# Normalising with the mean itself instead of a negated copy, in a one-core attention and expert kernel

## Chip, cores and metric

The kernel runs on one core of one Trainium2 chip. The metric is device time in microseconds (us), from start to end of one execution. A core has TensorE (PE, with its weight loads shown apart as PEld), VectorE (DVE), ScalarE (ACT), GpSimd (POOL) and SyncE (SP, which only issues DMAs here).

## The reference

One layer on x of 8 batches, 256 rows each, 256 features. The attention half is `x = x + LN(attention(LN(x)))` with 16 query heads, 4 key heads, head size 128, a layer norm and a rotation of q and k, a causal softmax and an output projection. The second half is `x = x + LN(ffn(LN(x)))`, where ffn is a top-2 choice of 8 experts and one shared expert. The plain layer norm of both halves has no gain:

```python
def _layernorm(x, axis=-1, eps=1e-05):
    m = jnp.mean(x, axis=axis, keepdims=True)
    v = jnp.var(x, axis=axis, keepdims=True)
    return (x - m) / jnp.sqrt(v + eps)
```

Everything is fp32. On TensorE each product is made of three passes (lines L460, L461, L462) over high and low parts of the operands, which is why DVE has many subtractions that make low parts (lines with W as output).

## The kernel before

All of x stays in SBUF as X, 128 rows by 256 columns in each of 16 tiles. The order of work of every engine is written out by hand, and the engines meet through semaphores. A woven loop over slots s = 0 to 128 carries the attention: slot by slot one head's scores, softmax, transposes, value product and output projection, and beside it the projection, norm and rotation of q and k of a coming (batch, key head) group. One such group has two units u, one for each tile of 128 rows. After slot 128 the tail of the attention is woven with the router, the scatter of rows to the experts and the first items of the shared expert; then come the expert tiles and the last norms.

Two of the layer norms are touched here, each once for a batch b of two tiles:

- ln1, before the attention. DVE takes statistics (`ln1_stats`, L1346 and L1350), which leaves mean and variance side by side in the tile `mv`, slots 0 and 1. POOL makes the factor 1/sqrt(var+eps) (`ln1_root`, L2005 to L2007, through `root`, L2000 and L2002) in the tile `lr`. Then X is normalised into `hrow`: by DVE for batch 0 (`ln1_apply`, L1358) and by POOL for batches 1 to 7 (`ln1_apply`, L2040). In the loop the POOL root stands in slot 16b-10 and the POOL apply in slot 16b-5.
- the norm of the attention's output, in place in `osb`: statistics on DVE (`out_stats`, L1488 and L1492) into slots 2 and 3 of `mv`, root on POOL (`out_root`, L2056 to L2058), scaling by POOL for batches 0 to 5 (`out_scale`, L2047) and by DVE for batches 6 and 7 (L1498), then the addition to X (`out_add`).

On POOL these stand in one queue with `rope(u)`, four large or middling operations for each unit (L2002, L2016, L2019, L2026) and one small one (L2000), and later with the scatters (`scatter`, L2111, an indirect DMA issued by POOL). POOL's form of the normalisation adds a negated mean, which it first makes in a tile of its own, `nm`; DVE's form of the same subtracts the mean in `mv`. The router's work on DVE after the loop (`route_count`, `place_own`, `place_ends`, L1631 to L1669) stands ahead of `out_scale(6)` and of `pv_lo(58)` (L1478), which makes an operand that TensorE needs.

Of the kernel before, what the change touches and what calls it, by code (L numbers as in the profile page):

```python
# [5 lines left out]
ALU = mybir.AluOpType  # L6
# [109 lines left out]
def program(nc, x_d, wqkv_d, wo_d, gb_d, sw_d, ew_d, cs_d, const_d, route_d, spare_d, out_d):  # L116
    with ExitStack() as ctx:
        def sb(name, shape, dt=F32):
            return ctx.enter_context(nc.sbuf_tensor(name, shape, dt))
# [4 lines left out]
        def sem(name):  # L124
            return ctx.enter_context(nc.semaphore(name))
# [10 lines left out]
        X = sb("X", [128, NT, HID])  # L136
# [20 lines left out]
        hrow = sb("hrow", [128, 2, HID])  # L157
        p_flat = sb("P", [128, 1536])
        P = p_flat[:, :].rearrange("p (z c) -> p z c", z=4)
        osb = sb("osb", [128, 2, HID])  # L160
# [7 lines left out]
        st = sb("st", [128, 4, 6])  # L168
        mv = sb("mv", [128, 4, 2])
        lr = sb("lr", [128, 4])  # L170
        nm = sb("nm", [128, 4])
        nmx = sb("nmx", [128, 4, 2])
        sums = sb("sums", [128, 4, 2])
        rinv = sb("rinv", [128, 4, 2])
# [37 lines left out]
        for c, (a, b) in enumerate(CHUNKS):  # L212
# [60 lines left out]
                for (a, b), p in zip(CHUNKS, (pQ[:, 768:1024], pS[1], pS[1]))]  # L273
# [44 lines left out]
        s_bn, s_aggr, s_hrow, s_hT, s_wsum, s_wmean_d, s_wcen, s_wqlo_d, s_tab_d, s_rope_d = (  # L318
            sem(n) for n in ("s_bn", "s_aggr", "s_hrow", "s_hT", "s_wsum", "s_wmean_d", "s_wcen", "s_wqlo_d",
                             "s_tab_d", "s_rope_d"))  # L320
# [5 lines left out]
        s_obn, s_oaggr, s_oscale, s_res = (sem(n) for n in ("s_obn", "s_oaggr", "s_oscale", "s_res"))  # L326
# [1669 lines left out]
        def _(e):  # L1996
            def root(n, src, dst, scale, s_of, s_variance, s_root, k):

                e.wait_ge(*s_of)
                e.tensor_scalar(dst, src, scale, EPS, ALU.mult, ALU.add).then_inc(s_variance, 1)  # L2000
                e.wait_ge(s_variance, k + 1)
                e.tensor_tensor(dst, dst, half[:, 0:n], ALU.pow).then_inc(s_root, 1)  # L2002

            def ln1_root(b):
                e.wait_ge(s_aggr, b + 1)  # L2005
                e.tensor_scalar(nm[:, 0:2], mv[:, 0:2, 0], -1.0, None, ALU.mult)
                root(2, mv[:, 0:2, 1], lr[:, 0:2], 1.0, (s_aggr, b + 1), s_var, s_lr, b)  # L2007

            def rope(u):
# [26 lines left out]
            def ln1_apply(b):  # L2036
                e.wait_ge(s_lr, b + 1)
                e.wait_ge(s_ln1T, b)
                for t in range(2):
                    a = e.tensor_scalar(hrow[:, t, :], X[:, 2 * b + t, :], nm[:, t:t + 1], lr[:, t:t + 1], ALU.add,  # L2040
                                        ALU.mult)
                a.then_inc(s_hrow, 1)

            def out_scale(b):
                e.wait_ge(s_olr, b + 1)
                for t in range(2):
                    a = e.tensor_scalar(osb[:, t, :], osb[:, t, :], nm[:, 2 + t:3 + t], lr[:, 2 + t:3 + t], ALU.add,  # L2047
                                        ALU.mult)
                a.then_inc(s_oscale, 1)

# [2 lines left out]
                e.tensor_tensor(X[:, 2 * b:2 * b + 2, :], X[:, 2 * b:2 * b + 2, :], osb[:, :, :], ALU.add).then_inc(s_res, 1)  # L2053

            def out_root(b):
                e.wait_ge(s_oaggr, b + 1)  # L2056
                e.tensor_scalar(nm[:, 2:4], mv[:, 2:4, 0], -1.0, None, ALU.mult)
                root(2, mv[:, 2:4, 1], lr[:, 2:4], 1.0, (s_oaggr, b + 1), s_ovar, s_olr, b)  # L2058

            def norm_root(k):  # L2060
# [110 lines left out]
            e.memset(half[:, :], -0.5).then_inc(s_half, 1)  # L2171
            e.wait_ge(s_half, 1)
            ln1_root(0)
            e.wait_ge(s_wqhi, 1)
            e.tensor_tensor(WQ[:, 0, 1, 0, :], raw_q[0][:, 0, :], f(WQ[:, 0, 0, 0, :]),
# [9 lines left out]
            for s in range(WOVEN):  # L2185
                if s == 2:
                    rope(0)
                if QFIRST <= s <= 2 * NU and (s - 1) % 2 == 1:
                    rope((s - 1) // 2)
                if s % 16 == 6 and s // 16 + 1 < NB:  # L2190
                    ln1_root(s // 16 + 1)
                fb, fs = divmod(s - LATE - 15, 16)
                if s % 16 == 11 and s // 16 + 1 < NB:
                    ln1_apply(s // 16 + 1)
                if 0 <= fb < NB - 1 and fs == 1:
                    out_root(fb)
                if 0 <= fb < NB - 2 and fs == 2:
                    out_scale(fb)
                if 0 <= fb < NB - 2 and fs == 4:
                    out_add(fb)  # L2200
                if 0 <= fb < NB - 2 and fs == 7:
                    ln2_root(fb)
                if s == ZERO:
                    row_ends()
                if s - 1 in SWHI[0:2]:
                    sw_lo(SWHI.index(s - 1))
# [37 lines left out]
            scatter(1, 11, 0)  # L2244
            scatter(1, 11, 1)
            out_root(7)
            e.wait_ge(s_uact, 4)
            scatter(1, 12, 0)
# [82 lines left out]
```

## Time and profile before

| what | value |
|---|---|
| median of 3 runs | 675.61 us (675.12 to 675.86) |
| the profiled execution's own time | 675.86 us |
| its span, first to last instruction | 673.9 us |
| mean granted TensorE clock | 0.977 of full speed |
| busy PE / DVE / ACT / POOL | 628.6 / 564.9 / 563.8 / 541.8 us |
| instructions on POOL | 606 |

The span is 1.96 us shorter than the time of the same execution; that rest lies outside the first and last instruction. Busy time of an engine says how full it is over the whole span, and not which engine sets the end in a stage: for that one reads the stretches, the waits and the chain that ended last. A duration in the trace runs from an instruction's start to its end, so an instruction that is held up after its start shows as a long one, and the time is not counted as idle.

### The profile page before, as it was taken

The numbers are of one execution on the slowest core, as the hardware profiler recorded it, in microseconds if no ns is written. First come the engines' busy times: TensorE is split into PE (matmuls) and PEld (weight loads), VectorE is DVE, ScalarE is ACT, GpSimd is POOL, SyncE is SP. The second block draws the span as 40 slices with busy tenths as digits, with TensorE's granted clock in tenths as the row PEclk, the third lists the DMA queues.
The fourth block names the chain that finished last, engine by engine and source line by source line (L and its number), as shares of the span: only waits on it lengthen the run. The fifth ranks groups of instructions, "written<-read, shape, count | busy, mean of one in ns | idle before, by whom it ended". The sixth has DMA issues, their size and how long they took to land.

```text
span 673.9 us, 15554 instructions
## 1 busy us (share of the span) xinstructions
PE 628.6 (93%) x4430; PEld 582.7 (86%) x4430; DVE 564.9 (84%) x1925; ACT 563.8 (84%) x2175; POOL 541.8 (80%) x606
## 2 busy tenths in 40 slices
PE   3678999999999999999999999999899999999993
PEld 2457899999999999999999999999789889999981
DVE  6899999998989899898988989988999855555576
ACT  5779999999999999999999999999898545666643
POOL 5799889899899989989989998999877424666654
PEclk9698999999999999999999999999899999999998
DMA  8000022999350000000000000000437124443263
GB/s 339 16 1 32 6 99 78 334 335 320 9 46 1 2 2 2 1 2 1 1 2 1 2 1 2 1 1 25 138 115 232 37 83 117 127 128 120 71 258 125
DMA packets 50979, 54.20 MB, mean 80 GB/s; under 512 B 19825, under 2 KB 42609, under 8 KB 50769
## 3 DMA queue, kind: packets, MB, share of 16 engines
q1 hardware_dynamic: 47488, 43.84, 22.2%
q0 software_dynamic: 3408, 9.38, 3.8%
q8 instruction: 38, 0.62, 0.4%
q14 instruction: 45, 0.36, 0.2%
HBM read 23.76 MB, written 29.51 MB: 79 GB/s over the span
## 4 chain that ended last, share of the span: by engine, by line
PE 80%; DVE 11%; ACT 4%; POOL 3%; issue 1%; DMA 1%; ACTq 0%; DVEq 0%; POOLq 0%
PE pQ L460 8%; PE pQ L461 8%; PE pQ L462 7%; PE pP L552 6%; PE pO L460 5%; PE pO L461 5%; PE pO L462 5%; PE pT L528 5%; PE pS L460 4%; PE pA L460 3%; PE pA L461 3%; PE pA L462 3%; PE pS L461 3%; PE pS L462 3%; PE pS L540 2%; PE pA L731 1%
## 5 line engine op out<-in xcount | busy, mean ns | idle before, releaser
L460 PE MATMUL pQ<-W 128*128 128x512 f32 (+2 forms) x334 | 119.4, 358 | 9.6 <-DVE W L1386 4.8
L992 ACT ACTIVATE P<-P,nmx 128x128 f32<-128x128 f32 (+1 forms) x256 | 119.0, 493 | 0.0
L461 PE MATMUL pQ<-W 128*128 128x512 f32 (+2 forms) x334 | 114.4, 343 | 0.0
L462 PE MATMUL pQ<-W 128*128 128x512 f32 (+2 forms) x334 | 114.0, 341 | 0.0
L2016 POOL TENSOR_TENSOR ropes<-ropes 128x640 f32<-128x640 f32 x63 | 99.0, 1571 | 12.3 <-DVE ropes L1442 12.0
L1000 ACT ACTIVATE P<-P,rinv 128x128 f32<-128x128 f32 (+1 forms) x256 | 106.1, 483 | 2.6 <-DVE rinv L1469 2.6
L2026 POOL TENSOR_TENSOR ropes<-ropes 128x640 f32<-128x640 f32 x63 | 99.4, 1578 | 4.9
L460 PE MATMUL pO<-W 128*128 128x256 f32 (+1 forms) x323 | 95.2, 295 | 5.1 <-DVE W L1478 3.6
L977 ACT ACTIVATE ropes<-pQ 128x128 f32<-128x128 f32 x320 | 88.8, 306 | 6.6 <-POOL ropes L2026 4.3
L461 PE MATMUL pO<-W 128*128 128x256 f32 (+1 forms) x323 | 91.8, 284 | 0.0
L462 PE MATMUL pO<-W 128*128 128x256 f32 (+1 forms) x323 | 91.5, 283 | 0.0
L1473 DVE TENSOR_TENSOR W<-pP,W 128x384 fp32r<-128x384 f32 x128 | 70.1, 548 | 22.3 <-ACT W L1005 22.2
L2019 POOL TENSOR_TENSOR ropes<-ropes,rs 128x640 f32<-128x640 f32 x63 | 82.3, 1306 | 4.9
L2002 POOL TENSOR_TENSOR rs<-rs,half 128x5 f32<-128x5 f32 x64 | 77.4, 1210 | 5.3
L460 PEld LDWEIGHTS pQ<-W 128*128 128x128 f32 x334 | 65.3, 195 | 16.3 <-issue 4.8
L977 ACT ACTIVATION_READ_ACCUMULATOR ropes<-pQ 128x1 f32 x320 | 75.6, 240 | 0.0
L460 PEld LDWEIGHTS pO<-W 128*128 128x128 f32 x323 | 61.6, 191 | 11.5 <-DVE W L1478 5.6
L462 PEld LDWEIGHTS pQ<-W 128*128 128x128 f32 x334 | 65.3, 196 | 6.0
L461 PEld LDWEIGHTS pQ<-W 128*128 128x128 f32 x334 | 65.6, 196 | 2.7
L1005 ACT ACTIVATE W<-pP 128x384 fp32r<-128x384 f32 x128 | 66.2, 517 | 1.7 <-PE pP L552 1.6
L528 PE MATMUL pT<-const,ropes 128*128 128x128 f32 x320 | 58.0, 280 | 7.9 <-DVE W L1452 7.5
L2140 POOL DMA_INDIRECT ys<-ropes x39 | 38.8, 995 | 33.1 <-ACT ropes L1128 18.0
(270 smaller groups left out, 2197.4 us busy)
## 6 DMA issues: line engine op xcount, KB each, us to landing
xs<-stage SPq DMA_DIRECT2D x1, 17550.0 KB, 58.4
stage<-xs SPq DMA_DIRECT2D x39, 130.0 KB, 2.3
ropes<-in_ew SPq DMA_DIRECT2D x8, 608.0 KB, 4.8
stage<-in_wqkv SPq DMA_DIRECT2D x3, 768.0 KB, 8.6
stage<-ys SPq DMA_DIRECT2D x4, 512.0 KB, 6.2
ropes<-ys SPq DMA_DIRECT2D x4, 512.0 KB, 7.4
out<-X SPq DMA_DIRECT2D x7, 256.0 KB, 2.0
X<-in_wo SPq DMA_DIRECT2D x1, 1536.0 KB, 13.0
```

Source lines behind the costliest of these rows:

```text
L460: e.matmul(out, lh, rh, start=start, stop=False, skip_group_check=True)
L461: e.matmul(out, lh, rl, start=False, stop=False, skip_group_check=True)
L462: return e.matmul(out, ll, rh, start=False, stop=stop, skip_group_check=True)
L528: p = e.transpose(pT[:, i * 128:i * 128 + 128], t1[:, u % 3, (h0 + i) * D:(h0 + i) * D + D], ident)
L977: a = e.activation(t2[:, z, h * D:h * D + D], pQ[:, h * D:h * D + D], ACT.Square, accum_out=ss[:, z, h:h + 1])
L992: a = e.activation(P[:, z, span(t)], P[:, z, span(t)], ACT.Exp, bias=nmx[:, z, t:t + 1], scale=-1.0, accum_out=sums[:, z, t:t + 1])
L1000: a = e.activation(P[:, z, span(t)], P[:, z, span(t)], ACT.Copy, scale=rinv[:, z, t:t + 1])
L1473: e.tensor_tensor(PT[:, 1, n % 2, :], pP[:, 0:384], f(PT[:, 0, n % 2, :]), ALU.subtract).then_inc(s_PT, 1)
L2002: e.tensor_tensor(dst, dst, half[:, 0:n], ALU.pow).then_inc(s_root, 1)
L2016: e.tensor_tensor(t1[:, z3, :], t1[:, z3, :], t2[:, z, :], ALU.add).then_inc(s_add, 1)
L2019: e.tensor_tensor(v3, v3, rs[:, z, :].unsqueeze(2).to_broadcast([128, 5, D]), ALU.mult).then_inc(s_mul, 1)
L2026: e.tensor_tensor(v3, v3, TB[:, t, :, :], ALU.add).then_inc(s_rope, 1)
```

## The change

POOL no longer makes the negated mean. The tile `nm` goes, `ln1_root` and `out_root` each lose one instruction (and the wait ahead of it, which `root` repeats), and POOL's two normalising instructions subtract the mean from `mv` where they added the negated one from `nm`. Tiles allocated after `nm` move down in SBUF.

```diff
@@ program
-        nm = sb("nm", [128, 4])
@@ gpsimd
             def ln1_root(b):
-                e.wait_ge(s_aggr, b + 1)
-                e.tensor_scalar(nm[:, 0:2], mv[:, 0:2, 0], -1.0, None, ALU.mult)
                 root(2, mv[:, 0:2, 1], lr[:, 0:2], 1.0, (s_aggr, b + 1), s_var, s_lr, b)
@@ ln1_apply
-                    a = e.tensor_scalar(hrow[:, t, :], X[:, 2 * b + t, :], nm[:, t:t + 1], lr[:, t:t + 1], ALU.add,
+                    a = e.tensor_scalar(hrow[:, t, :], X[:, 2 * b + t, :], mv[:, t, 0:1], lr[:, t:t + 1], ALU.subtract,
                                         ALU.mult)
@@ out_scale
-                    a = e.tensor_scalar(osb[:, t, :], osb[:, t, :], nm[:, 2 + t:3 + t], lr[:, 2 + t:3 + t], ALU.add,
+                    a = e.tensor_scalar(osb[:, t, :], osb[:, t, :], mv[:, 2 + t, 0:1], lr[:, 2 + t:3 + t], ALU.subtract,
                                         ALU.mult)
@@ 
             def out_root(b):
-                e.wait_ge(s_oaggr, b + 1)
-                e.tensor_scalar(nm[:, 2:4], mv[:, 2:4, 0], -1.0, None, ALU.mult)
                 root(2, mv[:, 2:4, 1], lr[:, 2:4], 1.0, (s_oaggr, b + 1), s_ovar, s_olr, b)
```

## Rows read from the trace of the kernel before

**Rows 1.** Busy time of the loop's stretch: span, then busy us and instructions per engine, clock, DMA:

```profile
84.00:470.00 386.00, 385.48 (x2843) 364.24 (x2842) 347.54 (x1295) 368.89 (x1544) 353.84 (x363) 1.00 0.21 56
```

**Rows 2.** The negations of both roots: duration min/median/max, first and last start:

```profile
L2006 POOL TENSOR_SCALAR nm<-mv x8: 217/218/808, 5.4 to 387.0; 128x2 f32<-128x2 f32 x8
L2057 POOL TENSOR_SCALAR nm<-mv x8: 221/223/1229, 128.0 to 520.7; 128x2 f32<-128x2 f32 x8
```

**Rows 3.** POOL by line: count | busy us, mean ns | idle before:

```profile
L2016 POOL TENSOR_TENSOR ropes<-ropes 128x640 f32<-128x640 f32 x63 | 99.0, 1571 | 12.3 <-DVE ropes L1442 12.0
...
L2002 POOL TENSOR_TENSOR lr<-lr,half 128x2 f32<-128x2 f32 x24 | 18.1, 754 | 2.0
...
L2104 POOL TENSOR_TENSOR W<-stage,W 128x704 fp32r<-128x704 f32 x2 | 3.4, 1707 | 0.0
```

**Rows 4.** Timeline of the start: start us, us, engine, line, operation:

```profile
6.24 0.83 DVE L1381 TENSOR_TENSOR stage<-stage,wmean 128x640 f32<-128x640 f32 x1
...
6.98 0.73 DVE L1358 TENSOR_SCALAR hrow<-X,mv,lr 128x256 f32<-128x256 f32 x2
```

**Rows 5.** The same view, 37 to 48 us:

```profile
37.81 1.84 DVE L1386 TENSOR_TENSOR W<-stage,W 128x768 fp32r<-128x768 f32 x1
...
38.92 0.81 POOL L2006 TENSOR_SCALAR nm<-mv 128x2 f32<-128x2 f32 x1
...
39.79 0.19 POOL L2000 TENSOR_SCALAR lr<-mv 128x2 f32<-128x2 f32 x1
...
43.91 1.26 POOL L2019 TENSOR_TENSOR ropes<-ropes,rs 128x640 f32<-128x640 f32 x1
...
44.68 3.25 DVE L1381 TENSOR_TENSOR stage<-stage,wmean 128x640 f32<-128x640 f32 x2
...
45.25 2.00 POOL L2026 TENSOR_TENSOR ropes<-ropes 128x640 f32<-128x640 f32 x1
```

**Rows 6.** Chain that ended last, 42 to 84 us, the pieces around DVE's run:

```profile
42.24 0.02 issue
...
83.33 0.51 PE pA L460
```

**Rows 7.** Timeline, 473 to 483 us:

```profile
473.43 0.22 POOL L2057 TENSOR_SCALAR nm<-mv 128x2 f32<-128x2 f32 x1
...
477.86 1.26 POOL L2019 TENSOR_TENSOR ropes<-ropes,rs 128x640 f32<-128x640 f32 x1
...
478.44 0.70 DVE L1635 CAST csum<-stage 128x8 fp32r<-128x8 f32 x1
...
479.19 1.57 POOL L2026 TENSOR_TENSOR ropes<-ropes 128x640 f32<-128x640 f32 x1
...
479.64 1.16 DVE L1666 TENSOR_SCALAR stage<-stage 128x10 f32<-128x10 f32 x1
...
482.24 0.39 PE L460 MATMUL pO<-W 128*128 128x256 f32 x1 [2.81 <-DVE W L1478]
```

**Rows 8.** Busy time by stretch, where the clock falls:

```profile
481.00:484.00 3.00, 1.76 (x11) 1.76 (x12) 2.97 (x8) 1.27 (x4) 2.20 (x2) 0.85 0.75 206
484.00:487.00 3.00, 3.00 (x16) 2.83 (x15) 2.03 (x10) 1.86 (x3) 2.42 (x5) 0.58 1.01 382
```

**Rows 9.** Timeline, 520 to 525 us:

```profile
520.72 1.23 POOL L2057 TENSOR_SCALAR nm<-mv 128x2 f32<-128x2 f32 x1
...
522.01 0.36 POOL L2000 TENSOR_SCALAR lr<-mv 128x2 f32<-128x2 f32 x1
...
522.35 1.16 DVE L1517 TENSOR_TENSOR W<-ropes,W 128x960 fp32r<-128x960 f32 x1
...
522.46 1.64 POOL L2002 TENSOR_TENSOR lr<-lr,half 128x2 f32<-128x2 f32 x1
...
524.13 0.74 DVE L1498 TENSOR_SCALAR osb<-osb,mv,lr 128x256 f32<-128x256 f32 x2 [0.19 <-POOL lr L2002]
```

**Rows 10.** Waits of all engines, 516 to 560 us:

```profile
PE pS L460 <- DVE stage L1575: 1.1, 1, 1.1
```

## The prediction

> **What bounds the kernel now.** I read the busy time by stretch first, since one share over the whole span hides the stages. In the long stretch of the attention loop PE is busy 385.48 of 386.00 us at full clock [rows 1]: nothing that POOL does faster there can end anything sooner, as long as PE's operands still come in time. Then the removed instructions themselves, for their durations: 16 of them, median about 0.22 us, with two far longer ones, 808 and 1229 ns [rows 2]. A two-column operation that takes 1.2 us is not computing; the question is what holds it, and whether that thing is on the path. Third, the chain of waits that ended last, to find the stages where PE is not the bound: from 42.26 to 83.3 us it is DVE without a gap, 41 us, between the two pieces shown [rows 6], and around 480 us PE stands 2.81 us for one DVE subtraction [rows 7]. Last, the timelines around the 16 instructions in those stages, where DVE and POOL block one another. A DVE operation of 640 columns takes 0.83 us alone [rows 4], and two of them took 3.25 us at 44.68, while POOL had 128x640 operations of its own in flight [rows 5]. So in the stages where DVE sets the pace, when POOL starts an instruction matters though POOL is not the bound.
>
> **The arithmetic of the change.** 16 negations go. Fourteen at some 0.22 us make 3.1 us, with the two long ones 5.1 us of POOL's busy time. None is the time gained; each place is looked at by itself. The subtraction in place of the addition I cost at nothing: POOL's 704-column subtraction takes 1707 ns, 2.42 ns a column, its 640-column operation, an addition, 1571 ns, 2.45 ns a column [rows 3], and DVE's form of both normalisations already subtracts from `mv` [rows 4, 9]. Should it cost more, all 14 `hrow` and 12 `osb` instructions of POOL but the two of batch 1 at 54 us lie under a fully busy PE. The mean is held in `mv` longer than before, and its next writer on DVE stands behind work that needs the finished `hrow` or `osb`, so I see no new wait. The move of some small tiles by 16 bytes I put at nothing too; no row shows a price for an address.
>
> **Batch 0, at 5.4 us.** The root comes 0.28 us sooner (0.22 for the instruction and 0.06 between two instructions, as from 39.73 to 39.79 in rows 5). DVE applies it only after its own L1381, which runs from 6.24 to 7.07, and the row of L1358 that makes `hrow` shows no wait for the factor [rows 4]: the factor lay ready before DVE was. Gain 0; a loss is excluded too, because nothing on POOL stands nearer to DVE's work than before except the power, and that one was short here already.
>
> **Batch 1, at 38.92 us (term A).** The negation took 0.81 us, since DVE's L1386 (37.81 to 39.65) ran until just before it ended [rows 5]. Without it L2000 takes its place, is held to the same moment, and everything behind it on POOL comes earlier by one small instruction, 0.28 us. DVE is not moved at first: its run begins at 42.26 behind an ACT instruction. At 44.68 it reaches L1381, which stands until POOL's L2019 is done at 43.91+1.26=45.17; then POOL's L2026 at 45.25 is held by DVE's first operation, takes its 1.56 us, ends at 47.25, and only then can DVE's second go, to 47.93 [rows 5]. All three hand-overs come 0.28 us earlier: L2019 ends at 44.89, still behind DVE's arrival at 44.68, so the whole 0.28 passes to DVE. From there DVE's run has no gap to 83.29 us [rows 6] which could swallow it, and POOL is moved by the same amount, so their order stays. Term A: -0.28 us, bounds 0 and -0.28 for this mechanism.
>
> **Batches 2 to 7 of ln1 and 0 to 5 of the output norm.** 12 negations between 84 and 470 us, 0.22 to 0.32 us each. PE has 0.52 us of idle time in all of this stretch [rows 1], which bounds the gain; the rope operations that would feed it sooner are not what it waits for. I take 0. POOL's freed 2.7 us become idle time. What is late next is nothing: the cover is PE's own queue.
>
> **Batch 6 of the output norm, at 473.43 us (term B).** Here the cover is gone. PE waits 2.81 us, until 482.24, for L1478; DVE comes to it late because L1635, an operation on 8 columns, took 0.70 us and ended when POOL's L2019 ended (477.86+1.26=479.12), and L1666, 10 columns, took 1.16 us and ended when L2026 ended (479.19+1.57=480.76) [rows 7]. Both POOL operations are behind the negation in the queue, with nothing idle between. Moved 0.28 us ahead they end at 478.84 and 480.48. DVE stands before both by then (it came to L1635 at 478.41), so it gets all 0.28 us, and PE with it. Term B: -0.28 us, bounds 0 and -0.28.
>
> **Batch 7 of the output norm, at 520.72 us (term C).** The negation was held 1.2 us by a DVE operation of 960 columns, L2000 after it 0.36, the power L2002 1.64 us by the second such, L1517 at 522.35; DVE then waited 0.19 us for the factor at 524.13 [rows 9]. The naive reading is that 1.23 us goes. It does not: L2000 would be held by the same DVE operation, to the same moment, 521.95. What changes is that the power is now ready at about 522.05, ahead of DVE's L1517 (522.35) and not behind it (522.46). An unheld power takes 0.71 us (24 of them have a mean of 754 ns, and without the one of 1640 ns it is 715 [rows 3, 9]). If POOL gets in, it runs from 522.3 to 523.0 and L1517 stands until then: L1517 ends 0.7 us later and L1498 starts at 524.6 for 524.13, a loss of about 0.45 us on DVE, whose 0.19 us of waiting and some slack take the rest. PE waits 1.1 us behind DVE's L1575 some 3 us later [rows 10], and DVE has no gap between, so PE gets what DVE gets. If DVE gets in first as before, only the 0.19 us of waiting goes. Bounds +0.45 and -0.19. I take +0.45, because the order read off the times of rows 9 gives it.
>
> Of the port I know only what these rows show, that a small instruction of either engine ends when the large one of the other ends. The Trainium skill, SBUF — State Buffer, section "Who interferes with whom", says that a DVE instruction with two SBUF inputs contends with GpSimd's reads, that the holder keeps the shared pair for the whole instruction, and that "Issue order, not op shape, decides who blocks". By that rule a shorter POOL queue can make DVE later, which speaks against this change; rows 5, 7 and 9 agree with it, each with an 8- to 960-column operation held to the other's end. Left out, term C is -0.19 and the sum -0.75; with it, -0.11.
>
> **The sum.** 0 - 0.28 + 0 - 0.28 + 0.45 = -0.11 us. Against the profiled execution, 673.9 us of span and 1.96 around it, that is 675.75. That execution lies 0.25 us above the median of the runs, so the forecast is 675.61 - 0.11 = 675.5 us.
>
> **Rivals.** (1) C without the turn-over: -0.28-0.28-0.19 = -0.75, so 674.9 us. For it: POOL and DVE are some tenths of a microsecond apart, less than what A and B may move them against DMA and ACT. (2) All is cover: whatever A and B save is spent waiting for ACT, whose chain stands beside DVE's in both places; 675.6. Against it: no ACT piece in 41 us of chain. (3) The clock. The PE clock was granted at 0.85 and 0.58 of full in the two stretches from 481 to 487 us, right after the stand of 2.81 us [rows 7, 8]. At the lower of its two levels (1.2 for 2.4 GHz) that makes 0.9 + 2.5 = 3.4 us, in which 1.7 us of work at full clock was done. If a stand of 2.53 us does not bring the clock down, up to 1.7 us more is gained: 673.8 us. Against it: the stand is shortened by only a tenth of itself. (4) Slower: the turn-over of C happens in the gapless DVE run between 42 and 84 us too. There the POOL operation that gets in ahead is a 128x640 one, and DVE stands its whole 1.57 us [rows 3] with nothing to absorb it: 675.5 + 1.57 = 677.1 us. It decides where POOL was ready less than 0.28 us behind a two-input DVE instruction. Against it: after 45 us both engines are moved alike, and between 39 and 44.7 DVE works from PSUM, where I see no held instruction.
>
> **Numbers.** Forecast 0.46; (1) 0.20; (2) 0.14; (3) 0.10; (4) 0.10. A measurement of this kernel tells a change from none beyond about 0.2%, 1.35 us: below 674.26 or above 676.96. Only (3) lies below, with a little of (1)'s spread, 0.14; only (4) above, 0.10; within, 0.76. The range reaches from half-way into (3), 673.9, over the spread of the runs shown (0.74 us), to most of the way to (4), 676.6.
>
> **What would show it.** The two root groups lose L2006 and L2057 and POOL falls from 606 to 590 instructions and by some 5 us if the hold-ups do not move to others; I expect L2000 and L2002 to take up 1.5 us of it. Two L1381 in one group near 44.7 us should take 2.97 and not 3.25 us. PE's longest wait for L1478 should be near 2.5 and not 2.81 us, followed by the same fall of the clock. Near 522 us, the power should be short (0.7 us) and L1517 behind it long (1.9 us) if C is right; both as before if rival (1) is. A PE that is no longer full between 84 and 470 us, or a DVE group in 42 to 84 us that is 1.5 us longer, would make the prediction wrong.

## The result and the profile after

The changed kernel takes 679.90 us (679.14 to 681.01, 4 runs) against 675.39 us (675.12 to 675.86, 4 runs) on the same chip: ratio 1.0065, 95% interval 1.005 to 1.008, 4.5 us slower. The forecast was 675.5 us, 0.11 under a median of 675.61, with a range from 673.9 to 676.6. It was wrong, in size and in sign. (The table of the kernel before has three of these four runs.) The profiled execution took 680.0 us with a span of 677.7.

The page of the kernel after begins with the engines' busy time and, in its fourth part, the chain of work that ended last:

```profile
PE 631.1 (93%) x4430; PEld 582.2 (86%) x4430; DVE 564.6 (83%) x1925; ACT 565.3 (83%) x2175; POOL 554.9 (82%) x590
...
POOL 55%; PE 26%; ACT 8%; DVE 5%; issue 4%; DMA 0%; ACTq 0%; DVEq 0%; POOLq 0%
```

POOL has 16 instructions fewer and is busy 13.1 us longer (541.8 before). Its share of the chain goes from 3% to 55%. POOL by line, busy us and mean ns, of the kernel after (L2013 is L2016 of before, L2037 is L2040, L2044 is L2047) shows where the added time lies:

```profile
L2013 POOL TENSOR_TENSOR ropes<-ropes 128x640 f32<-128x640 f32 x63 | 99.3, 1577 | 6.2 <-DVE ropes L1441 6.2
...
L2037 POOL TENSOR_SCALAR hrow<-X,mv,lr 128x256 f32<-128x256 f32 x14 | 18.4, 1319 | 0.0
...
L2001 POOL TENSOR_TENSOR lr<-lr,half 128x2 f32<-128x2 f32 x24 | 17.3, 720 | 2.0
...
L2044 POOL TENSOR_SCALAR osb<-osb,mv,lr 128x256 f32<-128x256 f32 x12 | 14.6, 1228 | 0.7
```

The same two normalisations in the kernel before:

```profile
L2040 POOL TENSOR_SCALAR hrow<-X,nm,lr 128x256 f32<-128x256 f32 x14 | 8.9, 642 | 0.0
...
L2047 POOL TENSOR_SCALAR osb<-osb,nm,lr 128x256 f32<-128x256 f32 x12 | 6.6, 556 | 0.7
```

The 640-column addition is what it was [rows 3]. But a normalisation of 256 columns takes 1.23 us where it took 0.55 (the mean of `hrow` is higher by one instruction of batch 1 that is held in both kernels): 26 of them, 17.5 us more, for 5.2 us of negations saved (2.3 and 2.9 by line; the prediction had 5.1). The other rows nearly cancel: L1999 of `lr` takes 0.6 us more in all and L2001 of `lr` 0.8 less, where the prediction wanted 1.5 us more in the two. And POOL's idle time ahead of L2013 is halved, 12.3 to 6.2 us.

The same stretch as [rows 1], in parts, in the kernel after (span, then busy us and instructions for PE, PEld, DVE, ACT, POOL):

```profile
200.00:300.00 100.00, 99.93 (x732) 93.73 (x731) 88.91 (x332) 95.53 (x402) 94.91 (x93) 1.00 0.01 2
...
400.00:470.00 70.00, 68.98 (x501) 63.68 (x500) 62.83 (x227) 65.40 (x269) 65.17 (x61) 1.00 0.02 7
```

and of the kernel before:

```profile
200.00:300.00 100.00, 100.00 (x741) 94.64 (x740) 89.87 (x336) 96.00 (x403) 91.82 (x95) 1.00 0.01 2
```

PE is "busy" 99.9 of 100 us in a kernel that does 732 matmuls where the other did 741. The busy time of overlapping matmuls hides the loss; the count of instructions, and PEld's busy time, show it. Only from 400 to 470 us does PE show idle time, 1.0 us (none there before): the sign that the prediction named for being wrong.

How long a batch takes is read from POOL's own output norm, which comes once a batch. Kernel before:

```profile
186.74 1.10 POOL L2047 TENSOR_SCALAR osb<-osb,nm,lr 128x256 f32<-128x256 f32 x2
...
244.12 1.09 POOL L2047 TENSOR_SCALAR osb<-osb,nm,lr 128x256 f32<-128x256 f32 x2
```

Kernel after:

```profile
186.37 2.44 POOL L2044 TENSOR_SCALAR osb<-osb,mv,lr 128x256 f32<-128x256 f32 x2
...
244.41 2.44 POOL L2044 TENSOR_SCALAR osb<-osb,mv,lr 128x256 f32<-128x256 f32 x2
```

57.38 us against 58.04: 0.66 us lost in each batch. The waits of 190 to 361 us, three batches, name the path. Those that have POOL in them, kernel before, then after (who waited <- for whom: us, times, longest):

```profile
POOL ropes L2016 <- DVE ropes L1442: 2.8, 3, 0.9
POOL rs L2000 <- ACT ropes L977: 1.5, 3, 0.5
```

```profile
ACT ropes L976 <- POOL ropes L2023: 4.2, 6, 0.8
...
PEld pT L527 <- POOL ropes L2023: 1.6, 6, 0.3
```

Before, POOL waited for the others, 4.3 us in three batches, 1.4 in one: that was its spare time. After, the view shows no wait of POOL, and the others wait for it: ACT may square the heads of unit u only when POOL has ended unit u-2, and PE transposes only what POOL has ended. The sum of one batch closes: four instructions longer by 0.67 are 2.7 us, two negations of 0.28 us less, so +2.13 us for 1.43 us of room; 0.70 us should show, and 0.66 do.

The delay can be followed through a kernel by the start of the same softmax instruction (DVE L1459 of the kernel before, 128 of them) in each profile, less its start in the profile of before. Worked out from the timelines:

| at (us, before) | 57 | 73 | 188 | 302 | 388 | 417 | 447 | 504 | end |
|---|---|---|---|---|---|---|---|---|---|
| after | -1.40 | -0.81 | -0.60 | 0.74 | 2.07 | 3.33 | 4.25 | 3.93 | 3.8 |
| add_mv | -0.26 | -0.27 | -0.24 | -0.22 | -0.22 | -0.17 | 0.89 | 0.72 | 0.7 |
| neg2 | 1.45 | 1.44 | 1.53 | 1.58 | 1.59 | 2.13 | 2.51 | - | - |
| neg4 | 2.81 | 2.80 | 3.76 | 5.36 | 6.94 | 8.24 | 9.26 | 10.29 | 12.2 |
| sub_ln1 | -1.07 | -0.38 | -0.37 | -0.34 | -0.34 | 0.60 | 0.60 | - | - |
| sub_out | -0.01 | -0.01 | 0.21 | 0.49 | 0.78 | 1.66 | 2.40 | - | - |
| sub_nm | 0.50 | 1.10 | 1.84 | 4.40 | 6.70 | 7.19 | 8.61 | 9.32 | 9.6 |
| dve_neg | -1.07 | -1.09 | 0.86 | 1.94 | 2.11 | 3.26 | 3.91 | - | - |
| dead | -0.02 | 0.00 | 0.03 | 0.06 | 0.08 | 0.09 | 0.11 | - | - |
| add_mv_b5 | -1.17 | -1.17 | -1.17 | -1.15 | -1.16 | -1.17 | -1.31 | - | - |
| after_again | -0.31 | 0.29 | 0.50 | 1.89 | 3.22 | 4.48 | 5.41 | - | - |

The level at 57 us also differs between executions of the same instructions by up to 1.1 us (after and after_again), so only differences along a row are read. The runs from neg2 and the halves on stood on chips where the kernel before itself took 681.2 to 681.8 us. On such a chip dead, which keeps to the kernel before within 0.2 us until 500 us, ends 5.6 us later: what these chips are slower by lies in the tail. Their last columns are left out, and each ratio below is against before on the same chip.

### The profile page after: what moved, and what is told of

The parts are those of the page before. It is cut to its first block, busy times and chain, and to the rows that moved or that the text cites. A ratio compares the mean times of both kernels' runs of the same rounds, so it can differ in the third digit from the quotient of the medians.

```text
span 677.7 us, 15538 instructions
## 1 busy us (share of the span) xinstructions
PE 631.1 (93%) x4430; PEld 582.2 (86%) x4430; DVE 564.6 (83%) x1925; ACT 565.3 (83%) x2175; POOL 554.9 (82%) x590
## 4 chain that ended last, share of the span: by engine, by line
POOL 55%; PE 26%; ACT 8%; DVE 5%; issue 4%; DMA 0%; ACTq 0%; DVEq 0%; POOLq 0%
POOL ropes L2023 12%; POOL ropes L2013 12%; POOL ropes L2016 10%; POOL rs L2001 9%; POOL hrow L2037 3%; PE pQ L459 2%; PE pQ L461 2%; PE pQ L460 2%; POOL osb L2044 2%; PE pO L459 2%; ACT ropes L976 2%; POOL rs L1999 2%; PE pO L460 2%; PE pO L461 2%; ACT P L991 2%
## 5 line engine op out<-in xcount | busy, mean ns | idle before, releaser
L2013 POOL TENSOR_TENSOR ropes<-ropes 128x640 f32<-128x640 f32 x63 | 99.3, 1577 | 6.2 <-DVE ropes L1441 6.2
L2016 POOL TENSOR_TENSOR ropes<-ropes,rs 128x640 f32<-128x640 f32 x63 | 81.2, 1290 | 4.9
L2001 POOL TENSOR_TENSOR rs<-rs,half 128x5 f32<-128x5 f32 x64 | 77.4, 1209 | 5.3
L551 PE MATMUL pP<-const,P 128*128 128x128 f32 x384 | 63.5, 275 | 1.3 <-DVE W L1472 1.2
```

The lines of the kernel that those rows point to most:

```text
L2013: e.tensor_tensor(t1[:, z3, :], t1[:, z3, :], t2[:, z, :], ALU.add).then_inc(s_add, 1)
L2016: e.tensor_tensor(v3, v3, rs[:, z, :].unsqueeze(2).to_broadcast([128, 5, D]), ALU.mult).then_inc(s_mul, 1)
```

## The experiments

**The operator or the operand (add_mv).**

```diff
-  e.tensor_scalar(hrow[:, t, :], X[...], mv[:, t, 0:1], lr[:, t:t + 1], ALU.subtract, ALU.mult)
+  e.tensor_scalar(hrow[:, t, :], X[...], mv[:, t, 0:1], lr[:, t:t + 1], ALU.add, ALU.mult)
   (the same in out_scale)
```

> The changed kernel with ALU.add in place of ALU.subtract in POOL's 26 normalisations (the mean is added, not subtracted: that part of the computation is changed), negations still gone, mean still read from mv. Theory 1 (the pair subtract, mult is the slow thing on POOL): the normalisation takes about 0.55 us as before, POOL falls to about 537 us busy, and the time is what the blind sum said, about 675.3 (675.4 - 0.1). Theory 2 (reading the mean from mv, with its 8-byte step, is slow): it takes 1.2 us and the time stays near 679.9.

Measured: 676.09 against 675.93 us, ratio 1.0003 (0.9994 to 1.0012). POOL by line:

```profile
L2037 POOL TENSOR_SCALAR hrow<-X,mv,lr 128x256 f32<-128x256 f32 x14 | 8.9, 645 | 0.0
...
L2044 POOL TENSOR_SCALAR osb<-osb,mv,lr 128x256 f32<-128x256 f32 x12 | 6.6, 560 | 0.7
```

It is the operator. Reading the mean from `mv` costs nothing, and neither do the moved tiles, which this kernel has too; the negations are gone as the change wanted, and that buys no time that can be measured. The row of the table shows why it does not keep the 0.2 to 0.3 us that it holds until 417 us: it loses 1.06 us between 417 and 447 (below).

**The other way round (sub_nm).**

```diff
-  e.tensor_scalar(nm[:, 0:2], mv[:, 0:2, 0], -1.0, None, ALU.mult)
+  e.tensor_scalar(nm[:, 0:2], mv[:, 0:2, 0], 1.0, None, ALU.mult)
-  ... nm[:, t:t + 1], lr[:, t:t + 1], ALU.add, ALU.mult)
+  ... nm[:, t:t + 1], lr[:, t:t + 1], ALU.subtract, ALU.mult)
   (the same in the output norm)
```

> The kernel before, where POOL copies the mean into nm (times 1.0 instead of -1.0) and subtracts it from nm. Theory 1: 1.23 us for each normalisation, POOL's load grows by 4 x 0.67 = 2.7 us in each batch of 57.2 us, where it had some 1.4 us of idle time; the rest, 1.3 us, is lost in each of about six batches, so about 675.4 + 8 = 683 us, slower than the changed kernel by the negations, some 3 us. Theory 2: 0.55 us each and 675.4 us.

Measured: 684.96 against 675.93 us, ratio 1.013 (1.0115 to 1.0146), 9.0 us slower; `hrow` at 1317 ns and `osb` at 1236 ns. In the table it loses 2.56 us in the two batches from 188 to 302 us, 1.28 a batch, where 2.7 - 1.4 = 1.3 was expected.

**The operations by themselves (ops).** Four of each behind DVE's last addition, for example

```diff
+            for i in range(4):
+                e.wait_ge(s_neg, 4 + i)
+                e.tensor_scalar(osb[:, 0, :], osb[:, 1, :], nm[:, 2:3], lr[:, 2:3], ALU.subtract, ALU.mult).then_inc(s_neg, 1)
```

> The kernel before, and at POOL's end, after DVE's last addition, 15 operations on osb four times each: tensor_scalar with the pairs (add, mult), (subtract, mult), (mult, add), (mult, subtract), (mult, mult) from two columns, three pairs from constants, single subtract and add, a single mult, tensor_tensor add and subtract, all 256 columns, and the first two pairs on 32 columns. Theory 1: (add, mult) 0.55 us, (subtract, mult) about 1.23 us alone too; if it is a matter of columns, the 32-column ones differ by an eighth of 0.67, 0.08 us; tensor_tensor is the same for both. Rival (the 1.23 us come from contention with DVE in the loop): both 0.55 us here. The single subtract has no row yet: 0.5 or 1.2 us.

Measured, POOL by line from 668 us on (busy us, mean ns), costliest first:

```profile
L2266 POOL TENSOR_SCALAR osb<-osb,nm,lr 128x256 f32<-128x256 f32 x4 | 4.9, 1228 | 0.4
L2272 POOL TENSOR_SCALAR osb<-osb,nm,lr 128x256 f32<-128x256 f32 x4 | 4.9, 1222 | 0.4
L2281 POOL TENSOR_SCALAR osb<-osb 128x256 f32<-128x256 f32 x4 | 4.3, 1071 | 0.3
L2293 POOL TENSOR_SCALAR osb<-osb,nm 128x256 f32<-128x256 f32 x4 | 3.7, 926 | 0.4
L2290 POOL TENSOR_SCALAR osb<-osb,nm 128x256 f32<-128x256 f32 x4 | 3.7, 921 | 0.4
L2287 POOL TENSOR_SCALAR osb<-osb 128x256 f32<-128x256 f32 x4 | 3.4, 850 | 0.3
L2299 POOL TENSOR_TENSOR osb<-osb 128x256 f32<-128x256 f32 x4 | 2.4, 612 | 0.3
L2296 POOL TENSOR_TENSOR osb<-osb 128x256 f32<-128x256 f32 x4 | 2.4, 611 | 0.3
L2269 POOL TENSOR_SCALAR osb<-osb,nm,lr 128x256 f32<-128x256 f32 x4 | 2.2, 558 | 0.4
L2275 POOL TENSOR_SCALAR osb<-osb,nm,lr 128x256 f32<-128x256 f32 x4 | 2.2, 555 | 0.4
L2263 POOL TENSOR_SCALAR osb<-osb,nm,lr 128x256 f32<-128x256 f32 x4 | 2.2, 554 | 2.5 <-DVE X L1753 2.2
L2305 POOL TENSOR_SCALAR osb<-osb,nm,lr 128x32 f32<-128x32 f32 x4 | 1.9, 474 | 0.4
L2284 POOL TENSOR_SCALAR osb<-osb 128x256 f32<-128x256 f32 x4 | 1.6, 404 | 0.3
L2278 POOL TENSOR_SCALAR osb<-osb 128x256 f32<-128x256 f32 x4 | 1.6, 403 | 0.3
L2302 POOL TENSOR_SCALAR osb<-osb,nm,lr 128x32 f32<-128x32 f32 x4 | 1.5, 364 | 0.4
```

With two columns as operands, (add, mult) L2263, (mult, add) L2269 and (mult, mult) L2275 take some 555 ns, but (subtract, mult) L2266 and (mult, subtract) L2272 some 1225. With constants the pairs (add, mult) L2278 and (mult, add) L2284 take 403, (subtract, mult) L2281 1071. One operation alone takes longer than a pair of add and mult, whichever it is: mult by a constant L2287, subtract L2290, add L2293. `tensor_tensor` is the same for add L2296 and subtract L2299. DVE, ACT and PE had ended their work (the last of DVE at 669 us), so it is not contention with them. This kernel ran once (725.71 us); only these rows of it are used. From 32 to 256 columns (add, mult) grows from 364 to 554 ns, 0.85 ns a column, (subtract, mult) from 474 to 1228, 3.4 ns a column.

**Load alone, without the slow pair (neg4, neg2).** Each negation 4 or 2 times more, POOL's normalisation as before.

```diff
+            def again(cols):
+                for _ in range(4):     (neg2: range(2))
+                    negs[0] += 1
+                    e.wait_ge(s_neg, negs[0])
+                    e.tensor_scalar(nm[:, cols], mv[:, cols, 0], -1.0, None, ALU.mult).then_inc(s_neg, 1)
+                negs[0] += 1
...
+                again(slice(0, 2))     (in out_root: slice(2, 4))
```

> The kernel before with each negation done five times over (four more of 0.28 us in both roots, 2.2 us more of POOL work in a batch), fast add form kept. Theory 1, second half (POOL has 1.4 us to spare in a batch, and what is above it goes into the time): 0.8 us lost in a batch, about 675.4 + 5 = 680.4 us, with ACT waiting for POOL's last rope operation. Rival (PE is full in the loop and POOL is hidden, what the blind prediction said; the 4.5 us come from something else in the change): 675.4, within 0.5.

Measured: 688.38 against 675.93 us, ratio 1.0189 (1.0175 to 1.0202), 12.4 us slower. The part in the loop is as expected: 0.80 us a batch (3.76 to 5.36 in two), with ACT waiting for POOL. The loss was expected at 5 us, 7.4 too low: the first and last roots lie outside the loop, and the row has 2.8 us lost by 57 us and 2.9 behind 447; the rest is the loop's last batches, 2.3 us from 388 to 447.

```profile
ACT ropes L977 <- POOL ropes L2036: 8.4, 9, 1.3
```

(Waits of neg4, 190 to 361 us; L2036 is L2026 of before.)

> The kernel before with each negation done three times over, 4 x 0.28 = 1.1 us more POOL work in a batch. With four more it lost 0.8 us in each batch, and 2.3 us at the start and some 3 us behind the loop. Threshold theory: nothing in a batch, half of the start's and the tail's losses, so 675.9 + 2.7 = 678.6 us. Rival (no threshold, in proportion): half of 12.45, 682.1 us.

Measured: 685.17 against 681.15 us, ratio 1.0051 (1.0033 to 1.0069), 4.0 us slower, where 2.7 were expected and 6.2 by the rival; but between 188 and 388 us it loses 0.06 us in all. So 1.1 us more in a batch is all but free and 2.2 us more costs 0.8: the loss is not in proportion, and it starts where POOL's idle time of 1.43 us puts it: 2.13, 2.24 and 2.7 us of added work less 1.43 are 0.7, 0.8 and 1.3 us a batch, and after, neg4 and sub_nm lose 0.67, 0.80 and 1.28 (188 to 302 us).

**Each half of the change (sub_ln1, sub_out).** The diff of the change for one norm only.

> Half of the change: ln1 without its negation and with (subtract, mult) from mv in POOL's 14 hrow instructions; the output norm as before. POOL's load in a batch grows by 2 x 0.67 - 0.28 = 1.07 us, less than the 1.4 us that it idles in a batch. Theory (POOL's spare time is a threshold): no loss in a batch, the time within 0.8 us of before, 675.5 to 676.7. Rival (each slow instruction costs its share of the whole 4.5 us): about 2.3 us slower, 678.2.

> The other half: the output norm without its negation and with (subtract, mult) from mv in POOL's 12 osb instructions; ln1 as before. Same load, 1.07 us a batch. Threshold theory: no loss in a batch, within 0.8 us of before, 675.5 to 676.7; the two halves' losses together are then less than the whole's. Rival: about 2.2 us slower, 678.1.

Measured: 682.38 and 681.76 against 681.15 us, ratios 1.002 (1.0007 to 1.0033) and 1.0009 (0.9993 to 1.0026). The first, 1.2 us, is outside the 0.8 us expected; the second is not told from no loss. Each adds 1.07 us to a batch. In the table sub_ln1 loses 0.03 us from 188 to 388 us, sub_out 0.57, the whole 2.67: there the halves together cost less than a quarter of the whole. Outside this stretch they do not behave so: from 388 to 447 us they lose 0.94 and 1.62 us, the whole 2.18. The totals cannot be set against the whole's 4.5 us, which was measured on another chip (2.6 us in after_again).

sub_out's 0.16 us a batch was expected at nothing. Its waits, 190 to 361 us:

```profile
ACT ropes L977 <- POOL ropes L2026: 2.4, 6, 0.5
POOL ropes L2016 <- DVE ropes L1442: 1.6, 3, 0.6
```

ACT waits for POOL while POOL still waits 0.5 us a batch for DVE. So the threshold is not sharp. By these waits the place in the batch at which the work is added counts too: some of POOL's idle time lies where the added work cannot use it. No run moves the work about to test this.

**The negation on DVE (dve_neg).**

```diff
   (DVE, behind bn_aggr)
+  e.wait_ge(s_aggr, b + 1)
+  e.tensor_scalar(nm[:, 0:2], mv[:, 0:2, 0], -1.0, None, ALU.mult).then_inc(s_nm, 1)
   (POOL)
-  e.tensor_scalar(nm[:, 0:2], mv[:, 0:2, 0], -1.0, None, ALU.mult)
```

> What the change may have wanted, without the slow pair: DVE makes the negated mean (a 2-column operation, 0.15 us) right behind its statistics for the 13 batches that POOL normalises, POOL keeps (add, mult) from nm and has no negation. POOL's load falls by 0.56 us a batch, DVE's grows by 0.3 of some 57. Theory (PE sets the loop as long as POOL stays under it): 675.9 + 0 within 1.3 us, with a turn of the order at the port worth up to 1.2 us either way near 422 us. Rival (POOL's queue limits the loop before too): 6 x 0.56 = 3.4 us faster, 672.5.

Measured: 685.09 against 681.15 us, ratio 1.0054 (1.0033 to 1.0075), 3.9 us slower; neither theory. DVE's negations are not 0.15 us long:

```profile
L1355 DVE TENSOR_SCALAR nm<-mv x7: 571/596/1078, 33.8 to 384.6; 128x2 f32<-128x2 f32 x7
L1500 DVE TENSOR_SCALAR nm<-mv x6: 1072/1074/1077, 124.6 to 414.4; 128x2 f32<-128x2 f32 x6
```

The timelines of that run show why:

```profile
182.56 1.07 DVE L1500 TENSOR_SCALAR nm<-mv 128x2 f32<-128x2 f32 x1
...
182.35 1.26 POOL L2024 TENSOR_TENSOR ropes<-ropes,rs 128x640 f32<-128x640 f32 x1
```

The DVE operation ends at 183.63, with POOL's at 183.61, and all 13 end within 0.05 us of the end of a 640-column operation of POOL. A two-column `tensor_scalar` of DVE takes 0.16 us where nothing holds it (L1666 at 539.25 us in the kernel before), so of the 1.67 us a batch that the two take, an estimate of 1.35 is standing for the port. How much comes through differs: 0.54 us a batch from 188 to 302 us, 0.17 in the one and a half batches to 388. The Trainium skill, SBUF — State Buffer, section "Who interferes with whom", counts `tensor_scalar` among the operations that can take the shared pair; the trace agrees.

**Only the negations that nobody reads (dead).** Batch 0 of ln1 and batches 6 and 7 of the output norm are normalised by DVE, from `mv`.

```diff
+                if b > 0:       # out_root: if b < 6
                     e.tensor_scalar(nm[:, 0:2], mv[:, 0:2, 0], -1.0, None, ALU.mult)
```

> The kernel before without the three negations that nobody reads: batch 0 of ln1 and batches 6 and 7 of the output norm, which DVE normalises from mv. The loop is left alone. Theory: nothing at the start and in the loop; the stand of PE at L1478 near 482 us falls by 0.28 us (term B of the prediction), and at 522 us either 0.2 us is gained or 0.45 lost; so -0.5 to +0.2 us against before. Rival (the negations' full time, 0.2 + 0.2 + 1.2 us, comes off): -1.6 us.

Measured: 680.96 against 681.81 us, ratio 0.9987 (0.9973 to 1.0), 0.85 us faster where 0.5 at most was expected; the interval covers both. PE's longest wait for L1478 is 2.6 us for 2.81. Of the kernels that still subtract the mean it is the only one with a ratio under 1, and its interval touches 1.

**The order at the port near 422 us (add_mv_b5).**

```diff
   (add_mv, in out_root)
+  if b == 5:
+      e.tensor_scalar(nm[:, 2:4], mv[:, 2:4, 0], -1.0, None, ALU.mult)
```

> The (add, mult) form on mv without negations (the mean is added, not subtracted: that part is changed), but with one idle negation put back, in the output norm's root of batch 5, near 415 us. Theory: with POOL's rope end 0.3 to 0.4 us later, DVE's L1599 (the router's 80-column product near 422 us) gets the port first again and takes 0.3 and not 1.44 us; the 1.1 us that the run without it lost between 417 and 447 us is not lost. Rival (that loss has nothing to do with the order at the port): it stays.

Measured: 680.48 against 681.81 us, ratio 0.9981 (0.9966 to 0.9995). This kernel too adds the mean. DVE's router lines in the timelines of add_mv, where 640-column operations of POOL had begun at 421.57 and 425.80:

```profile
421.81 1.44 DVE L1599 TENSOR_TENSOR stage<-stage 128x80 f32<-128x80 f32 x1
...
425.97 1.49 DVE L1605 SCALAR_TENSOR_TENSOR stage<-stage 128x80 f32<-128x80 f32 x1
```

and of add_mv_b5, where DVE comes first, before POOL's 420.98 and 425.22:

```profile
420.85 0.24 DVE L1600 TENSOR_TENSOR stage<-stage 128x80 f32<-128x80 f32 x1
...
423.81 0.27 DVE L1606 SCALAR_TENSOR_TENSOR stage<-stage 128x80 f32<-128x80 f32 x1
```

One instruction of 0.3 us more on POOL makes two of DVE's 2.4 us shorter. From 417 to 447 us the run gains 0.14 us where add_mv lost 1.06. It was foretold, so the order at the port is shown to be the cause of that loss.

**The change once more (after_again).** No edit.

> The changed kernel once more, beside before and the other two on this chip: 4 to 5 us slower than before, with 0.66 us lost in each batch from 190 to 390 us, if the first result belongs to the kernel and not to that chip.

Measured: 684.45 against 681.81 us, ratio 1.0035 (1.002 to 1.005), 2.6 us slower. Along the loop it repeats the first profile (1.39 us from 188 to 302 us, 1.34 in the first; 5.1 us from 73 to 447, 5.06 in the first), so the loss belongs to the kernel. The total is 2.6 us, less than the 4 to 5 expected: on this chip the tail is longer for both, and part of the delay must be absorbed there. Which wait absorbs it was not settled.

## Why the prediction was wrong

**The step that failed: "The subtraction in place of the addition I cost at nothing".** It measured 0.67 us more for each of 26 instructions. The rows behind it were `tensor_tensor` [rows 3], whose two forms do cost the same (611 and 612 ns), and DVE's `tensor_scalar`. No row had a POOL `tensor_scalar` with a subtraction in a pair. That was an operation which the trace did not show, and it should have had a bound above: the nearest row in time per column, 2.45 ns of the 640-column addition, gives 0.63 us for 256 columns against 0.55, and even that bound is too low for the 1.23 us found.

**The second step: "Should it cost more, all ... lie under a fully busy PE".** The cover was finite, and its size stood in the trace: POOL waited 12.0 us for DVE ahead of its 63 rope additions [rows 3], and the waits of 190 to 361 us give 1.4 us a batch with those for ACT. neg2 and neg4 measure this room from both sides, the halves less sharply. PE's 385.48 of 386 us [rows 1] was no evidence: after the change it is 99.9 of 100 too from 200 to 300 us. Both failures were needed: with 0.55 us the load falls and nothing is lost in the loop (add_mv, 0.02 us from 188 to 388 us).

**Term A, -0.28 us: right.** The two L1380 of add_mv take 2.96 us for 3.25 [rows 5], those of the changed kernel 2.97. Along the rows DVE's starts come 0.30 us (add_mv) and 0.29 us (after) sooner between 44 and 46 us; the -0.27 of the table alone would show nothing, since the level varies by more. In the changed kernel the gain is given back at once: 0.59 us are lost between 57 and 73 us, inside the stretch where DVE had no gap [rows 6], and PE stands for batch 1's slow `hrow`, the two instructions which the prediction had left uncovered:

```profile
56.68 0.65 PE L473 MATMUL pA<-const,hrow 128*128 128x128 f32 x4 [1.12 <-POOL hrow L2037]
```

**Batch 0: 0, right.** From 4 to 8 us DVE's distance to the kernel before moves from -0.25 to -0.24 us in the changed kernel and from 0.02 to -0.01 in add_mv.

**Term B, -0.28 us: right where it acts.** Between 478 and 482 us DVE's starts come 0.29 us sooner in the changed kernel, 0.26 in add_mv and 0.25 in dead, and PE waits 2.5 us for 2.81 [rows 7] (2.6 in dead). By 490 us 0.33 us of it are left in the changed kernel, 0.17 in add_mv and nothing in dead.

**Term C, +0.45 us: wrong in sign.** Between 520 and 524 us five kernels without this negation (after, after_again, add_mv, dead, sub_out) gain 0.27 us each, somewhat beyond the lower bound of -0.19. Less of it reaches the end: from 504 us on the changed kernel regains 0.17 us and add_mv 0.03, since both lose 0.2 to 0.4 us between 640 and 660 us, which no run explains. The turn of the order did come, but it held nobody. The changed kernel's timeline at this place:

```profile
525.46 0.25 POOL L1999 TENSOR_SCALAR lr<-mv 128x2 f32<-128x2 f32 x1
...
525.79 0.90 POOL L2001 TENSOR_TENSOR lr<-lr,half 128x2 f32<-128x2 f32 x1
...
526.14 1.16 DVE L1516 TENSOR_TENSOR W<-ropes,W 128x960 fp32r<-128x960 f32 x1
```

DVE's 960-column operation takes its usual 1.16 us though the power started 0.35 us ahead of it, and so it does in add_mv and dead. A power that needs the port for only a part of its time would do this; no run shows which part. By the Trainium skill, SBUF — State Buffer, section "Who interferes with whom", the holder keeps the shared pair for the whole instruction, as the prediction has it; that does not fit here, and the measurement decides. Where the holder is one of the 640-column operations the rule fits (dve_neg, add_mv).

**Rivals.** (1), C without the turn-over, had all three terms nearly right where they act, and would have been the forecast for a subtraction that costs nothing; add_mv shows the three, but ends 0.7 us behind the kernel before for the losses near 422 us and between 640 and 660 us. (4) named the mechanism of that loss, DVE standing one rope operation long, but placed it between 42 and 84 us; it struck the router's DVE work in the loop's last batches, 1.2 us twice. (3), the clock, came in one profile of two: in the changed kernel's first it fell behind the stand as before, in after_again, behind a stand of the same 2.5 us, it did not. That execution regains 0.66 us from 478 to 490 us and the first 0.33, so the clock was worth some 0.3 us there and not 1.7. The length of the stand alone does not decide whether it falls. Busy time by stretch of after (a share of 0.50 is the lower of the two levels, 1.2 of 2.4 GHz), then of after_again (the share is the third number from the end):

```profile
488.00:491.00 3.00, 3.00 (x13) 2.73 (x12) 2.50 (x13) 2.38 (x6) 2.47 (x5) 0.50 0.96 371
...
489.00:492.00 3.00, 2.74 (x20) 2.28 (x18) 2.83 (x16) 2.18 (x5) 2.35 (x4) 1.00 1.00 375
```

None of the rivals was a POOL queue that becomes the bound in the loop, and that is what happened.

Left open: why the slow pair costs more in the last batch (1.3 us between 388 and 417 us in the changed kernel, 0.9 in each half, which loses little or nothing in the batches before).

## What to carry to other kernels

Before an engine's work is called hidden, write down how long it waits for others in one period of the loop; that number, and not the bound engine's busy share, is what an added cost is held against. Well below it a cost was all but free here (0 to 0.16 us of 1.1), above it the excess was paid in each period. An operation whose operator pair no row shows is an unknown cost even if it looks like its neighbour. Fewer instructions are not less work until the remaining ones have been timed. Where two engines share a port, a saving of 0.3 us can turn an order and cost 1.

## What the runs showed of the hardware

- POOL's `tensor_scalar` on 128x256 fp32 (ops): pairs of add and mult 0.55 us with operands from columns and 0.40 with constants; a pair with a subtraction 1.23 and 1.07; a single operation 0.85 to 0.93, more than a pair of add and mult. A single multiplication is dearer than a multiplication and an addition.
- POOL's `tensor_tensor` on 256 columns takes 0.61 us, add or subtract.
- DVE's `tensor_scalar` of two columns takes 0.57 to 1.08 us when POOL has a 640-column operation under way, and ends with it; 0.16 us otherwise.
- A DVE `tensor_tensor` of 960 columns takes 1.16 us beside a POOL power of two columns that started 0.35 us before it.
- After a stand of TensorE of 2.5 us the granted clock fell to 0.50 (its lower level) in one profile and stayed at 1.00 in another of the same kernel.
